# Masked keys, row places and scatter order in a three-layer hybrid block

## The reference

```python
x = x + window_attention(group_norm(x))      # 8x8 windows, shifted by 4, 8 heads of 16,
                                             # q and k normalised to unit length, learned bias, mask
t = x as (32, 1024, 128)
t = t + banded_attention(layer_norm(t))      # rows of 128 tokens, 4 heads, 0 <= i - j <= 32
t = t + experts(layer_norm(t))               # 8 experts, 128 -> 256 -> 128, exact GELU

def experts(xf):                             # every token: the two likeliest of 8 experts
    probs = softmax(xf @ gate_w + gate_b); top2_vals, top2_idx = top_k(probs, 2)
    return sum over e of weight[e] * (gelu(xf @ W1[e] + b1[e]) @ W2[e] + b2[e])
```

## Time and profile before

| | |
|---|---|
| median of three runs | 3139.29 us |
| the profiled execution | 3139.42 us |
| its span, first to last instruction | 3137.6 us |
| busy share: PE, DVE, POOL, ACT | 83%, 67%, 63%, 60% |
| mean granted share of PE's clock | 0.897 |
| DMA, mean over the span | 103 GB/s |

### The profile page before, as it was taken

The page is one execution under the profiler, slowest core; times in us unless marked ns, Lnnn a source line. Parts: engine busy times, 40 slices in busy tenths (PEclk is TensorE's granted clock), DMA queues, the critical chain, the costliest instruction groups (busy, mean ns, idle before and its releaser), DMA issues.

```text
span 3137.6 us, 76001 instructions
## 1 busy us (share of the span) xinstructions
PE 2607.6 (83%) x27338; PEld 1847.8 (59%) x27338; DVE 2107.0 (67%) x5357; ACT 1868.3 (60%) x3409; POOL 1986.5 (63%) x2221
## 2 busy tenths in 40 slices
PE   6888898998888888888888888888888888876773
PEld 3465555666666666566666656665656665654452
DVE  3578777786766676777667767677776677653333
ACT  3666666666666667666656666666666666553231
POOL 1335555555666777656667766667766677767765
PEclk8999988888999999898988998889898988888887
DMA  4011111113323232143333324344433343336674
GB/s 126 17 33 36 39 36 38 40 39 109 92 79 96 80 99 70 41 140 113 107 109 107 102 88 144 94 148 121 132 106 111 103 131 126 123 119 236 184 243 159
DMA packets 218931, 322.86 MB, mean 103 GB/s; under 512 B 39020, under 2 KB 138488, under 8 KB 213504
## 3 DMA queue, kind: packets, MB, share of 16 engines
q1 hardware_dynamic: 170368, 216.89, 22.7%
q0 software_dynamic: 38144, 78.72, 7.6%
q10 hardware_dynamic: 10048, 22.38, 2.3%
HBM read 205.64 MB, written 131.37 MB: 107 GB/s over the span
## 4 chain that ended last, share of the span: by engine, by line
PE 37%; POOL 28%; issue 14%; ACT 9%; DVE 7%; DMA 2%; SPq 1%; ACTq 1%; POOLq 0%; DVEq 0%
POOL y_tokens L1261 11%; POOL x_sorted L1251 9%; PE bank_m L860 4%; PE bank_s L824 4%; PE bank_to L784 3%; POOL km_a L1235 3%; PE bank_m L852 3%; PE bank_s L778 3%; POOL s_sb_b L1244 3%; POOL s_sb_a L1244 2%; PE bank_s L739 2%; PE bank_s L830 2%; PE bank_to L793 2%; PE bank_m L841 2%; ACT L1207 2%
## 5 line engine op out<-in xcount | busy, mean ns | idle before, releaser
L1261 POOL DMA_INDIRECT y_tokens<-yo,back_to x680 | 705.4, 1037 | 313.3 <-issue 144.9
L1251 POOL DMA_INDIRECT x_sorted<-xn_c,place_i x512 | 522.1, 1020 | 219.9 <-issue 134.9
L1244 POOL TENSOR_TENSOR s_sb_a<-s_sb_a,mx_a 128x512 f32<-128x512 f32 x256 | 268.7, 1050 | 532.4 <-DVE mx_a L1617 529.6
L1609 DVE TENSOR_TENSOR s_sb_a<-bank_s,bias_a 128x512 f32<-128x512 f32 x256 | 176.6, 690 | 340.5 <-PE bank_s L723 234.3
L852 PE MATMUL bank_m<-xe,wk_e 128*128 128x512 f32 x552 | 291.6, 657 | 36.4 <-ACT hid L1112 26.1
L723 PE MATMUL bank_s<-km_a,qk_a 32*64 32x128 f32 x4096 | 128.0, 305 | 202.9 <-POOL km_a L1235 141.3
L860 PE MATMUL bank_m<-wk_e,hid 128*128 128x128 f32 x2208 | 292.0, 297 | 1.2 <-ACT hid L1112 1.2
L860 PEld LDWEIGHTS bank_m<-wk_e,hid 128*128 128x128 f32 x2208 | 286.4, 213 | 2.6 <-issue 1.9
L1077 ACT ACTIVATE pt_sb_b<-bank_to 128x512 f32<-128x512 f32 x256 | 152.7, 596 | 218.8 <-PE bank_to L784 218.2
L1244 POOL TENSOR_TENSOR s_sb_b<-s_sb_b,mx_b 128x512 f32<-128x512 f32 x256 | 270.6, 1057 | 14.2 <-DVE mx_b L1617 14.0
L1235 POOL TENSOR_TENSOR km_a<-qk_a,k_consts 128x128 f32<-128x128 f32 x512 | 231.7, 475 | 45.3 <-DVE qk_a L1447 40.4
(11 more groups left out here) (231 smaller groups left out, 6375.2 us busy)
## 6 DMA issues: line engine op xcount, KB each, us to landing
wk_e<-in_w_experts_dram SPq DMA_DIRECT2D x134, 321.5 KB
xs<-x_sorted SPq DMA_DIRECT2D x134, 260.0 KB
yg<-y_tokens SPq DMA_DIRECT2D x26, 1024.0 KB
t_kept<-t SPq DMA_DIRECT2D x64, 256.0 KB, 2.2
xin<-in_x_dram SPq DMA_DIRECT2D x128, 112.0 KB
x_res<-in_x_dram SPq DMA_DIRECT2D x256, 56.0 KB
t_back<-t_kept SPq DMA_DIRECT2D x23, 512.0 KB, 4.2
out_dram<-yg SPq DMA_DIRECT2D x104, 112.0 KB
```

The source lines that it names most:

```text
L1244: pool.tensor_tensor(s[:, :, :], s[:, :, :], m[:, :, None].to_broadcast(shape), ALU.subtract).then_inc(s_sub[w], 1)
L1251: pool.indirect_dma_start(out=x_sorted[group_of[d] % XSIDES].ap(), out_offset=bass.IndirectOffsetOnAxis(ap=place_i[:, d % 2, n:n + 1], axi ...
L1261: pool.indirect_dma_start(out=y_tokens[pairs[u].group].ap(), out_offset=bass.IndirectOffsetOnAxis(ap=back_to[:, q % YO, j:j + 1], axis=0), ...
L1609: tt(s_sb[0][:, :, :].rearrange("p (r h) n -> p r (h n)", h=2), scores, bias_a[:, kind, :, :].rearrange("p (r h) n -> p r (h n)", h=2), AL ...
```

## The change

POOL's `masked_keys` is gone. DVE's `unit_vectors` writes each half image of keys twice, once for each head of a pair, with a scalar per partition that is the cap or zero; PE reads the masked keys from there and `km_ready` is gone. A row carries one number, HOME, the whole place of its output: it is written for the first choice, the eight scatters of the first choice go out, and when four of them have landed DVE writes the second choice's places over them (`second_homes`), for which POOL waits (`second`) before it scatters these. ACT copies the places of a tile's 512 slots into `back_to` behind `slots_copy`, into one of eight buffers, and DVE's L1580 is gone, as are the two gate instructions that made FIRST. `scattered` is split by halves of the image. The scatters are spread anew: steps 0 to 7 have 6, 5, 4, 3, 4, 6, 6 and 6, and an image's last one moves from (8, 3) to (10, 0).

```diff
-HOME, FIRST, ROW_W = D, D + 1, D + 2
+HOME, ROW_W = D, D + 1
 YO, MOVES = 3, PART * SUB
-BACK_AT = (((4, 1), (4, 1), (4, 2), (4, 3), (4, 3), (5, 0), (5, 1), (5, 2)),
+IDS = 8
+BACK_AT = (((4, 1), (4, 2), (4, 3), (4, 3), (5, 0), (5, 1), (5, 2), (5, 3)),
            ((6, 1), (6, 2), (6, 3), (7, 1), (7, 2), (7, 3), (8, 0), (8, 1)),
-           ((9, 1), (9, 2), (9, 3), (10, 1), (10, 2), (11, 0), (11, 1), (11, 2)))
-OUT_AT = ((5, 0), (5, 2), (5, 3), (6, 0), (6, 1), (6, 2), (6, 3), (7, 0), (7, 1), (7, 2), (7, 3),
-          (8, 0), (8, 1), (8, 2), (8, 2), (8, 3))
+           ((9, 1), (9, 2), (10, 0), (10, 1), (10, 2), (11, 0), (11, 1), (11, 2)))
+OUT_AT = ((5, 0), (5, 3), (6, 0), (6, 0), (6, 3), (7, 0), (7, 0), (7, 3), (8, 0), (8, 2), (8, 2), (8, 3),
+          (9, 0), (9, 0), (9, 3), (10, 0))
+OUT_ROWS = (4, 5, 6, 7, 0, 1, 2, 3)
...
-OWN_AT = B2_AT + D
-PACK_W = OWN_AT + 1
+PACK_W = B2_AT + D
...
-    put("pair_mask", ch[:, None] // DA % 2 == np.arange(2)[None])
+    put("pair_mask", NORM_CAP * (ch[:, None] // DA % 2 == np.arange(2)[None]))
...
-    spare = np.zeros((SPARE, ROW_W), np.float32)
-    spare[:, HOME] = TOP * np.arange(SPARE)
-    spare[:, FIRST] = E - 1
+    spare = np.zeros((2 * SPARE, ROW_W), np.float32)
+    spare[:, HOME] = np.arange(2 * SPARE)
...
-        qk_a = [sb(f"qk_a{n}", [P, 4, HALF]) for n in range(2)]
+        q_a = [sb(f"q_a{n}", [P, 2, HALF]) for n in range(2)]
+        kk_a = [sb(f"kk_a{n}", [P, 2, 2, HALF]) for n in range(2)]
         sq_a = sb("sq_a", [P, 4, HALF])
-        km_a = sb("km_a", [P, 2, 2, P])
...
-        back_to = sb("back_to", [P, YO, MOVES], U32)
+        back_to = sb("back_to", [P, IDS, MOVES], U32)
...
-                eng.wait_ge(scattered, 16 * TOP * TILES * (last_image[pair.group] + 1))
+                for h in range(2):
+                    eng.wait_ge(scattered[h], 16 * TILES * (last_image[pair.group] + 1))
...
-                    pe.wait_ge(km_ready, n + 1)
                     need(pe, qn_ready, a, 4, 2 + 2 * (ta // 4))
-                    q_flat = qk_a[a % 2][:, 0:2, :].rearrange("p a n -> p (a n)")
+                    q_flat = q_a[a % 2][:, :, :].rearrange("p a n -> p (a n)")
+                    keys = kk_a[a % 2][:, :, :, :].rearrange("p h a n -> p h (a n)")
                     for j in range(2):
                         for r in range(RG):
                             rows = slice(DB * r, DB * r + DB)
                             last = mm(S[r][WTOK * j:WTOK * j + WTOK, 0:P].rearrange("p (h n) -> p h n", h=2),
                                       q_flat[rows, window(2 * ta + j)],
-                                      km_a[rows, n % 2, :, WTOK * j:WTOK * j + WTOK], start=True, stop=True)
+                                      keys[rows, :, window(2 * ta + j)], start=True, stop=True)
...
+                for _, q, _ in pair.members:
+                    after(act, y_out[(q - IDS) % YO], 16 * MOVES * ((q - IDS) // YO + 1))
+                    func(back_to[:, q % IDS, :].rearrange("p (n j) -> p n j", n=PART), xs_b[buffer_of(q)[0]][:, :, :, HOME],
+                         ACT.Copy).then_inc(ids_kept, 1)
...
-            def masked_keys(n, h):
-
-                a, ta = tile_of(n)
-                steps_done(pool, s_ready[0], n - 1)
-                need(pool, qn_ready, a, 4, 1 + 2 * (ta // 4))
-                keys = qk_a[a % 2][:, 2 + ta // 4, P * (ta % 4):P * (ta % 4) + P]
-                op = pool.tensor_tensor(km_a[:, n % 2, h, :], keys, const("pair_mask")[:, h:h + 1].to_broadcast([P, P]),
-                                        ALU.mult)
-                if h == 1:
-                    op.then_inc(km_ready, 1)
...
+                t, choice = OUT_ROWS[n % TILES], n // TILES
                 pool.wait_ge(gate, GATE_STEPS * (d + 1))
+                if choice:
+                    pool.wait_ge(second, 2 * d + (1 if t >= 4 else 2))
                 if group_of[d] >= XSIDES:
                     pool.wait_ge(tile_t, last_tile[group_of[d] - XSIDES])
                 pool.indirect_dma_start(out=x_sorted[group_of[d] % XSIDES].ap(),
-                                        out_offset=bass.IndirectOffsetOnAxis(ap=place_i[:, d % 2, n:n + 1], axis=0),
-                                        in_=xn_c[d % 2][:, n % TILES, :], in_offset=None).then_inc(scattered, 16)
+                                        out_offset=bass.IndirectOffsetOnAxis(
+                                            ap=place_i[:, d % 2, TILES * choice + t:TILES * choice + t + 1], axis=0),
+                                        in_=xn_c[d % 2][:, t, :], in_offset=None).then_inc(scattered[t // 4], 16)
...
+                    pool.wait_ge(ids_kept, q + 1)
                     pool.wait_ge(yo_ready, q + 1)
                 j = k % MOVES
                 pool.indirect_dma_start(out=y_tokens[pairs[u].group].ap(),
-                                        out_offset=bass.IndirectOffsetOnAxis(ap=back_to[:, q % YO, j:j + 1], axis=0),
+                                        out_offset=bass.IndirectOffsetOnAxis(ap=back_to[:, q % IDS, j:j + 1], axis=0),
...
-                for h in range(2):
-                    if tiled(n + 1):
-                        masked_keys(n + 1, h)
...
-                    dve.wait_ge(scattered, 16 * TOP * TILES * (c - 1))
+                    dve.wait_ge(scattered[h], 16 * TILES * (c - 1))
...
-                cap = cols[:, 6:7] if n < 2 else NORM_CAP
-                here = qk_a[f % 2][:, n, :]
-                stt(here, sq_a[:, n, :], cap, here, ALU.min, ALU.mult).then_inc(qn_ready, 1)
+                if n < 2:
+                    here = q_a[f % 2][:, n, :]
+                    stt(here, sq_a[:, n, :], cols[:, 6:7], here, ALU.min, ALU.mult).then_inc(qn_ready, 1)
+                else:
+                    here = kk_a[f % 2][:, 1, n - 2, :]
+                    for h, keys in enumerate((kk_a[f % 2][:, 0, n - 2, :], here)):
+                        last = stt(keys, sq_a[:, n, :], const("pair_mask")[:, h:h + 1], here, ALU.min, ALU.mult)
+                    last.then_inc(qn_ready, 1)
...
+            def homes_of(d, choice, tiles):
+
+                first = last_image[group_of[d] - 1] + 1 if group_of[d] else 0
+                return ts(xn_c[d % 2][:, tiles, HOME], const("home")[:, tiles], float(TOP * TOKENS * (d - first) + choice),
+                          None, ALU.add)
...
-                stt(first_of, rank_c[:, :, :], 0.0, const("experts")[:, None, :].to_broadcast([P, TILES, E]),
-                    ALU.is_equal, ALU.mult).then_inc(gate, 1)
-                ts(here[:, :, HOME], const("home"), float(TOP * TOKENS * (d - first)), None, ALU.add).then_inc(gate, 1)
+                homes_of(d, 0, slice(0, TILES)).then_inc(gate, 1)
...
-                step(19)
-                dve.tensor_reduce(here[:, :, FIRST], first_of, AX_X, ALU.add).then_inc(gate, 1)
...
+            def second_homes(d, h):
+
+                dve.wait_ge(scattered[h], 16 * (TILES * d + 4))
+                homes_of(d, 1, slice(4 * h, 4 * h + 4)).then_inc(second, 1)
...
-                for h in range(PART):
-                    stt(back_to[:, q % YO, SUB * h:SUB * h + SUB], rows[:, h, :, FIRST], w[:, h, OWN_AT:OWN_AT + 1],
-                        rows[:, h, :, HOME], ALU.not_equal, ALU.add)
...
+                    if on(d - 1):
+                        second_homes(d - 1, 0)
...
+                    if on(d):
+                        second_homes(d, 1)
...
+            second_homes(IMAGES - 1, 0)
```

More of the change, by code:

```diff
@@ L129, in shape_constants @@
     put("base", rows(REGION * e))
-    put("experts", rows(e))
     put("home", TOP * (SPARE + TILES * ch[:, None] + np.arange(TILES)[None]))
@@ L1027, in layer_rstd, with queries_or_keys @@
                 func(rs[:, 1, :], rs[:, 0, :], ACT.Exp, scale=-0.5).then_inc(s, 1)
+            def queries_or_keys(f, w):
+                return flat(q_a[f % 2][:, :, :] if w == 0 else kk_a[f % 2][:, 1, :, :])
             def queries_keys(f, n):
                 need(act, s_ready[0], f - 2, TILES, TILES)
-                need(act, km_ready, f - 2, TILES, TILES)
                 need(act, qk_ready, f, 2, n + 1)
-                func(flat(qk_a[f % 2][:, 2 * n:2 * n + 2, :]), flat(bank_s[:, 2 * n:2 * n + 2, :]), ACT.Identity,
+                func(queries_or_keys(f, n), flat(bank_s[:, 2 * n:2 * n + 2, :]), ACT.Identity,
                      bias=cols[:, n:n + 1]).then_inc(qk_sb, 1)
@@ L1042, in squares @@
                 need(act, qn_ready, f - 1, 4, 4)
-                func(both(sq_a, w), both(qk_a[f % 2], w), ACT.Square).then_inc(sq_ready, 1)
+                func(both(sq_a, w), queries_or_keys(f, w), ACT.Square).then_inc(sq_ready, 1)
             def log_norms(f, w):
@@ L1764 @@
     b1 = b1.reshape(E, CH, P).transpose(0, 2, 1)
[L1765 to L1766 removed]
+    w_experts = np.concatenate([w1, w2, b1, np.repeat(b2[:, None, :], P, axis=1)], axis=2)
     arrays = dict(zip(_INPUTS, [
```

36 lines of the change are left out of this document (15 added, 21 removed).

## The result

The changed kernel took 3061.61 us (median of four runs, 3056.07 to 3066.29), the kernel before 3142.07 in the same rounds: a ratio of 0.9738, with a 95% interval of 0.9708 to 0.9768. The forecast of 3032 us was 30 us too low, inside its range. The profiled execution took 3065.05 us, its span 3063.2, which is 74.4 less than before. (Ratios here leave out runs over 1.5% above the fastest of the same kernel; where that matters, all runs are given.)

The account below looks back on a forecast made before the run. PE and POOL were taken to bound the kernel in turns, tied by the masks. Stretch and step 1 -131, passes without experts -25, indices +22, group loads +27 make -107 us: 3032 us, range 2940 to 3105.

Parts of the forecast that it names:

- the stretch from step 5 to step 0: Passes with three pairs: less POOL load shortens steps 5 through 0 by 4.2 us, 4.0 us in later passes.
- step 1's clock: Step 1 behind the stretch: PE's clock recovers once it no longer waits ahead, 2.5 us a pass, at most 5.0.
- the passes without experts: Passes 4 to 9, without expert tiles: POOL's stretch falls from 16 scatters to 12, gaining 25 us, ends 0 and 33.
- The zero end: Step 1: low end of its clock gain, nothing if POOL's subtraction takes the place of the mask.
- the head and tail: Only the tail was forecast: POOL's scatters one behind the other, 217.6 us, unchanged, with 10 us either way.
- the group changes: Loads at a change of group: later last scatter makes PE wait, 9 us each, 27 us lost, ends 0 and 36.
- ACT's indices: ACT's two index copies a pair, uncovered between steps 1 and 2, and 3 and 4: 22 us lost, ends 0 and 26.
- The rival that DVE becomes the bound in step 6: Step 6: added key instruction held up by POOL, 13 late passes lose 2.08 us each; 3059 us, chance 0.10.
- The slower case: Step 0: DVE held by second_homes when POOL's scatter at (7, 3) is late; up to 3178 us, chance 0.10.
- PE alone setting the pace: POOL and DVE leave the chain, step 1 gets its whole 5.0 us: 212 us gained, 2928 us, chance 0.20.
- that rival: PE's wait only moves, to POOL's subtraction at a step's end behind the same scatters: 3100 us, chance 0.05.

Follow-up runs that it names:

- e1: Kernel before with only the masks changed: POOL's masked_keys gone, DVE writes the keys twice; 2992.82 us, ratio 0.9515.
- e11: e1 with POOL again doing two 128x128 products a tile, into a tile nobody reads, PE not waiting for them; 3037.86 us, ratio 0.9673.
- e4: Changed kernel with the two scatters at (9, 0) moved to (9, 1), behind POOL's subtractions of step 1; 3007.60 us, ratio 0.9609.
- e9: Changed kernel with the edits of e3, e4, e5 and e6 together; 2946.80 us, ratio 0.9374.
- e3: Changed kernel with SP filling a new group's spare blocks ahead of its wait for the scatters; 3033.06 us, ratio 0.9658.
- e6: Changed kernel with the copy of the indices moved from ACT to DVE; 3055.63 us, ratio 0.9708.
- e5: Changed kernel with DVE's residual sum and statistics issued ahead of the masking of keys in step 6; 3056.61 us, ratio 0.9694.
- e10: e1 with the change's places for the 16 scatters of an image; 3006.70 us, ratio 0.9535.
- e12: Kernel before with DVE making the masked keys, statistics ahead of masking, spare rows first, and the change's places for the 16 scatters; 2988.15 us, ratio 0.9510.
- e13: Changed kernel with the edits of e3 and e4 together; 2973.88 us, ratio 0.9469.

## Why the prediction was right or wrong

**Right: the stretch from step 5 to step 0.** 81 us were forecast, 93.5 measured; 41.20 us in pass 14 lies 0.2 above the band of 39 to 41, 45.20 in pass 21 0.2 above that of 43 to 45. Its reason was only partly right. The prediction took POOL's load as the bound, and subtracted loads; e1 gets to 39.80 us with three scatters more, and e11 puts two thirds of what the masks gain on the wait itself and one third on the load. What held PE was standing behind POOL's queue more than how much was in it.

**Wrong: step 1's clock, and with it the passes without experts.** This is the step that failed: "I take half, 2.5 us" a pass, 50 us, and 25 us in passes 0 to 9. Measured were 6.0 and 8.7. The zero end was tied to POOL's subtraction taking the mask's place; that isn't what happened. With two scatters moved ahead of POOL's subtractions in step 1, DVE's normalisation was held up through them, PE waited for DVE, and its clock fell. With these two scatters behind the subtractions (e4) the two terms measured 30.4 and 24.0 us, and with the other three edits too (e9) 38.3 and 27.8: the second was about right in size, the first still too large. What was missing is that a transfer moved on POOL's queue has DVE as a neighbour: the prediction looked for such a hold in step 6 only.

**The sum.** That the gain in all came within 33 us of the forecast is partly luck. Step 1 and the passes without experts were 60 us short; the stretch, the indices and the head and tail together came out 34 us better than forecast, and step 3 6 us worse.

**Right: the group changes.** 9 us each were forecast, 9.7 on average came (29.0 in passes 10, 17 and 23), with 11.1 us of waits in pass 10. e3 shows the cause, and that the cost was one of order: the spare blocks needn't stand behind the scatters.

**Too dear: ACT's indices.** 22 us were forecast; steps 2 and 4 lost 9.5. One copy took 204 ns, the low end of the bracket (206), not the middle:

```profile
L1107 ACT ACTIVATE back_to<-xs 128x4 uint32<-128x4 f32 x156 | 24.0, 204 | 0.0
```

e6 does not tell this cost from what the copies cost on DVE.

**DVE.** L1580 is gone, and the 128 key instructions take 1033 ns on average and 743 in the median; e9, in another order, has 751 on average, so about a quarter of their time was hold. The rival that DVE becomes the bound in step 6 was a part of the outcome: step 6 of pass 21 takes 11.60 us with DVE busy for 11.49, and PE waits 27.7 us in all for the statistics. In pass 21 of after:

```profile
1734.14 3.40 DVE L1447 SCALAR_TENSOR_TENSOR kk_a<-sq_a,k_consts,kk_a 128x512 f32<-128x512 f32 x2
1737.46 0.68 DVE L1370 TENSOR_TENSOR t<-bank_s,t 128x512 f32<-128x512 f32 x1
1738.17 0.87 DVE L1376 BATCH_NORM_STATS2 st_c<-t 128x6 f32<-128x128 f32 x4
```

```profile
1733.72 1.05 PE L737 MATMUL bank_s<-wp_s,ot_b 128*128 128x128 f32 x8
1738.50 0.48 PE L721 MATMUL bank_s<-kk_a,q_a 32*64 32x128 f32 x16 [1.14 <-DVE st_c L1376]
```

The first two masking instructions take 3.40 us beside the end of a scatter and POOL's two subtractions (POOL from 1733.95 to 1736.98), though PE had the bank for L1370 ready at 1734.8, and PE then waits 1.14 us. But the gain of the stretch came through in spite of it, and e5 shows that taking this wait away alone returns little.

**The rivals that failed.** The slower case did not occur: up to pass 31 DVE never waited in `second_homes` (L1511; its first wait for a scatter comes at 2766 us). The only two waits of DVE for `x_sorted` up to 2600 us, 2.04 us each, stand in step 7 at the normalisation (L1384). PE alone setting the pace (2928 us) did not occur in after, but e9 comes within 19 us of it: what stood between was the order of work at a few places. The wait did not move as that rival had it: PE's waits for the exponential behind POOL's subtraction (`p_sb_a`) rose only from 25.1 to 38.8 us. But it did move in part, to places that no rival named: PE's idle time as a whole fell by 16.1 us where a wait of 141.3 had gone.

**Left open.** The places of the scatters cost 1.3 points in after (e4) and 0.2 to 0.6 on the kernels with the masks alone (e10, e12), but these are not the same edits: e4 moves two scatters, e10 and e12 move all 16. In step 1 alone the price is alike (40.7, 35.1 and 23.6 us in the profiled executions); what e10 and e12 gain in steps 0 and 7 by the same edit hides it. With the places alike, steps 6 and 7 together are 30.5 us longer in after than in e10. After differs there by the second choice's wait, the rows, ACT's copies and the places of the scatters back, and no run isolates which of these it is. Nor is it shown which of e9's last two edits gives its 1% over e13.

## What to carry to other kernels

When a wait is removed, look next at what then starts beside what: here 1.3 points of a gain were lost because two transfers, moved out of a crowded stretch, came to stand where they and what follows them hold up another engine. Split a change of many parts into its parts before trusting the sum: one clause gained more than the whole change, and two small moves gave back about what the others had lost (e13). When a step is moved, follow every later instruction of its queue, and ask whether work that needs nothing from it (the spare rows) can go ahead.

## What the runs showed of the hardware that was not expected

A tensor_scalar of 128x128 on DVE, 0.335 us at the median, took 2.61 to 2.82 us in the 19 cases in which it began inside a scatter that two POOL subtractions followed; the hold ran on from one POOL instruction into the next. Begun inside the second subtraction alone (e4), the same line took at most 1.03 us. In the kernel before, the same instruction (L1391), begun inside a scatter with a masked-key product behind it, took 0.88 us at most in 22 cases and ended before the product did. So not every POOL instruction carries the hold on; what decides it is not shown. DVE's additions from PSUM (L1612 of after) were never held: 670 ns at least, 693 at most in 256.
